# Tiles of x turned in memory ahead of time: the cross-attention scores read them by DMA, without transposes on TensorE

## The chip, the core and the metric

The kernel runs on one core of one Trainium2 chip. The metric is the device time of one launch in microseconds (us), as the median of several runs; less is better. The core's engines run side by side, each with an instruction queue of its own: TensorE (PE; its weight loads are PEld), VectorE (DVE), ScalarE (ACT), GpSimd (POOL) and SyncE (SP), which in this kernel only issues DMAs. They wait for each other by semaphores.

## What is computed

Eight batches of x (512 rows of 512 numbers) go through a cross attention over 77 context rows and then through a layer of 16 attention experts. Cut to what matters (`ln` is a layer norm over the row):

```python
ctx = ctx_1024                                           # (8, 77, 512)
s   = einsum('bqd,bkd->bqk', ln(x), ctx) / sqrt(512)
att = softmax(where(mask, -1e9, s), -1)
x   = x + swapaxes(att @ ctx, -1, -2) @ W_merge.T + b_merge
h   = ln(x)
rw  = gating(h)                                          # (8*512, 16) expert weights per row, in sequences of 512
q, k, v = [sum_e rw[.., e] * (h @ proj_e) for proj in (q_proj, k_proj, v_proj)]   # 64 wide
a   = causal_softmax(q k^T / 8) @ v
out = x + sum_e rw[.., e] * (a @ o_proj_e)
```

All products are taken in two parts: a tile `hi` rounded to the matmul's number format and a tile `lo` that holds the rest, as hi*hi + hi*lo + lo*hi.

## The kernel before

The rows of x are cut into 32 tiles of 128 rows, four to a batch. The main loop goes batch by batch (`body(b, ...)`); a batch has 32 slots k, eight to a tile (j, g = k // 8, k % 8). In slot k, TensorE first multiplies a tile of h with the projections of two experts (a **group**: 12 matmuls, L1213), and then does the small jobs that tables of numbers place in this slot: transposes, scores, values, mixing, output projection. Each engine's program is the same walk over the slots, so the tables set the order on every engine. Bodies for batches 0, 1, 6 and 7 are written out; one loop runs batches 2 to 5; a last body finishes the attention of batch 7. A small ramp ahead of the loop does the cross attention of the first five tiles and loads the weights.

The cross attention runs five tiles ahead (`X1_LEAD`). For one tile the steps are:

- SP loads the rows of x into H (`load_x1`, L393) as soon as TensorE has turned the h that lay in H (slot 6 of the tile before); the mask follows on L394.
- TensorE turns H, four transposes of 128x128 into one of two psum banks psT (`move_rows`, L1131, slot 0); ScalarE copies the bank to hT_hi (`copy_rows`, L615, slot 0) and VectorE takes bank minus hT_hi as hT_lo (`low_rows`, helper `lo`, L793, slot 0). L1131, L615 and L793 serve h in slot 6 of each tile in the same way.
- VectorE takes mean and variance from H in slot 3. TensorE forms the scores from hT and the turned context in slot 4 (`x1_score`, L1146 and L1148). Softmax and the low parts follow in slots 4 to 6.

The next tile of h is prepared in the same slots: `sum_x2` on TensorE and `add_x2` on VectorE (slot 2, L1163, L863), `row_stats` (slot 2, L868 and L870), powers on POOL (L504 to L515), `normalise` into H (slot 4, L874), transposes of H (slot 6).

For the batch after this one TensorE sums G = att^T times the merge weights, one quarter q in each of the slots 17, 19, 21 and 23 (`sum_G`, L1154). The merge weights come from a scratch in memory by DMA into one pair of buffers (`load_merge`, L400): the quarter q+1 is loaded when quarter q has been summed. SP walks the slots as well and waits in order. In slot 19 it first waits for `row_stats` of this tile (L383, store of X2), issues that store, a slice of the context (L379) and the next context (L448), and only then the merge load; in slot 21 it first waits for `normalise` (L387) and loads X2.

Of the kernel before, what the change touches and what calls it, by code (L numbers as in the profile page):

```python
# [37 lines left out]
QK_T_AT = {15: 0, 18: 1, 31: 2, 2: 3}  # L38
SCORES_AT = {18: 0, 20: 1, 2: 2, 4: 3}
GATES_AT = {19: 0, 21: 1, 3: 2, 5: 3}  # L40
PROBS_T_AT = {20: 0, 22: 1, 4: 2, 6: 3}
GATES_T_AT = {24: 0, 8: 1}
VALUES_AT = {24: 0, 8: 1}
MIX_AT = {26: (0, 0), 27: (0, 1), 28: (0, 2), 29: (0, 3),
          10: (1, 0), 11: (1, 1), 12: (1, 2), 13: (1, 3)}
MIX_LO_AT = {k + 1: job for k, job in MIX_AT.items()}
PROJECT_AT = {k + 2: job for k, job in MIX_AT.items()}
Y_AT = {31: 0, 0: 1, 15: 2, 16: 3}
# [5 lines left out]
X1_T_SLOT, X1_MOMENTS_SLOT, X1_SCORE_SLOT, X1_INV_SLOT, X1_LOW_SLOT = 0, 3, 4, 5, 6  # L54
# [42 lines left out]
def cross_attention_then_experts_kernel(nc, x, ctx_in, mask, merge_t, bias, sim, gates, w_qkv, w_o, out):  # L97
# [21 lines left out]
    with whole:  # L119
# [15 lines left out]
        with ExitStack() as under:  # L135
# [8 lines left out]
            cs_raw = raw("cs_raw", [CP, P])  # L144
        W_lo_over = sb("Wqkv_lo", [P, KC * W_CHUNK], F32R)
# [5 lines left out]
        cs_lo_over = sb("cs_lo", [CP, P], F32R)  # L151

# [32 lines left out]
        hT = [pair(f"hT{p}", [P, D]) for p in range(2)]  # L185
# [36 lines left out]
        x_first = [X2[:], resid[0][:], resid[1][:], spare_wo[:, 6, :], spare_wo[:, 5, :]]  # L222
        merge_first = ([mixedT[n // 2][:, n % 2 * 2:n % 2 * 2 + 2, :].rearrange("p c l -> p (c l)") for n in range(4)],
# [13 lines left out]
        ld_x = [sem(f"ld_x{n}") for n in range(X1_LEAD)]  # L237
        ld_mask = sem("ld_mask")
# [15 lines left out]
        x1_in = sem("x1_in")  # L254
# [27 lines left out]
        MOVES, HIS, OWN_STEPS = 36, 20, 4 * (3 + 5) + 4  # L282
# [38 lines left out]
        def tile_copies(k, qkv, lead):  # L321

            if k in QK_T_AT and (lead if k <= LATE_QK else qkv):
                return QK_T_AT[k]
            return None

        def bank_jobs(k, b, qkv, lead):


            j, g, prepare, cross, attn, ab = job_lists(k, b, qkv, lead)  # L330
            return ["probs"] * (attn and k in PROBS_T_AT) + ["x1"] * (cross and g == X1_T_SLOT) + [
                "sum"] * (prepare and g == SUM_SLOT) + ["score"] * (cross and g == X1_SCORE_SLOT) + [
                "h"] * (prepare and g == H_T_SLOT) + ["qk"] * (tile_copies(k, qkv, lead) is not None) + [
                "gates"] * (attn and k in GATES_T_AT) + ["ctx"] * (2 * (qkv and k == CTX_T_AT and live(b + 2, B))) + [
                "mix"] * (attn and k in MIX_AT)

# [24 lines left out]

        with nc.Block() as block:
            @block.sync
            def _(sp):
                moves = Seq()
                sp.dma_start(ctx_first[0], ctx_in[0]).then_inc(ld_ctx[0], 16)
                for n in range(TILES):
                    sp.dma_start(x_first[n], row(x, n)).then_inc(ld_x[n], 16)
# [43 lines left out]
                load_slice(0, 0)  # L412
                sp.dma_start(x_first[TILES], row(x, TILES)).then_inc(ld_x[TILES], 16)
# [13 lines left out]
                for _ in range(16):  # L427
# [7 lines left out]
                def body(b, qkv, lead):  # L435
                    for k in range(SLOTS):
                        j, g, prepare, cross, attn, ab = job_lists(k, b, qkv, lead)
                        t = TILES * b + j
                        for job in bank_jobs(k, b, qkv, lead):
                            n = moves.step()  # L440
                            if job == "h" and cross and live(t + X1_LEAD + 1, N_TILES):
# [35 lines left out]
            def _(pool):  # L477
# [91 lines left out]
                def body(b, qkv, lead):  # L569
                    for k in range(SLOTS):  # L570
# [12 lines left out]
                        if attn and k in GATES_AT:  # L583

                            i = GATES_AT[k]
# [785 lines left out]
```

## Time and profile before

| what | value |
|---|---|
| median of 3 runs | 947.69 us (947.27 to 949.32) |
| the profiled execution, its own time | 950.48 us |
| its span, first to last instruction | 948.8 us |
| TensorE busy, share of the span | 913.8 us, 96% |
| VectorE busy | 648.4 us, 68% |
| ScalarE busy | 213.4 us, 22% |
| mean granted TensorE clock, of full speed | 0.98 |
| matmuls of all kinds | 5128 |

The profile is one execution, taken by the hardware profiler. Busy times are unions, so matmuls that overlap in the pipeline count once. In the rows, L12 is line 12 of the kernel before; an arrow in brackets at the end of a row says for how long the engine had been idle and what released it. A row that names several instructions merges them.

### The profile page before, as it was taken

What the parts mean: (1) busy time and instruction counts of PE and PEld (TensorE: products, weight loads), DVE (VectorE), ACT (ScalarE), POOL (GpSimd) and SP (SyncE); (2) the same over time, 40 slices, a digit from 0 to 9 for tenths busy, and PEclk for the clock granted to TensorE, in tenths of its full rate; (3) what the DMA queues carried; (4) which work ended last, traced back from release to release, by engine and by line L of the source; (5) the groups of instructions that cost most, each with busy time, mean ns of one, the idle gap of its engine ahead of it and who ended that gap; (6) DMA issues with size and microseconds to landing.
All of it is one profiled execution on the core that took longest, in us unless ns stands there. A gap on an engine that the chain in (4) does not pass through costs nothing.

```text
span 948.8 us, 16504 instructions
## 1 busy us (share of the span) xinstructions
PE 913.8 (96%) x5128; PEld 853.4 (90%) x5128; DVE 648.4 (68%) x1964; ACT 213.4 (22%) x554; POOL 133.8 (14%) x383
## 2 busy tenths in 40 slices
PE   6779999999999999999999999999999999999987
PEld 5679899999999999999999999999999999999976
DVE  6778777767586675867667576876758676665743
ACT  4522321212122121212212131211312121121111
POOL 3243111101111110111111011110101110010100
PEclk9789999999999999999999999999999999999997
DMA  8821411224120331114111141112312131010110
GB/s 270 327 59 36 154 33 38 61 65 131 48 69 26 97 103 47 58 37 148 49 48 57 39 159 35 66 39 69 130 34 69 36 112 48 36 51 31 35 45 22
DMA packets 46086, 71.57 MB, mean 75 GB/s; under 512 B 9529, under 2 KB 16089, under 8 KB 45762
## 3 DMA queue, kind: packets, MB, share of 16 engines
q1 hardware_dynamic: 46018, 70.80, 22.9%
q8 instruction: 26, 0.43, 0.2%
q14 instruction: 42, 0.34, 0.1%
HBM read 51.90 MB, written 18.87 MB: 75 GB/s over the span
## 4 chain that ended last, share of the span: by engine, by line
PE 77%; DVE 8%; issue 6%; DMA 5%; SPq 2%; DVEq 1%; POOLq 1%; POOL 1%; ACT 0%; ACTq 0%
PE psQ L1213 44%; PE psO L1318 10%; PE psM L1318 9%; DMA merge_lo<-merge_scratch 3%; PE psT L1131 2%; PE psO L1154 2%; PE psM L1293 2%; PE psT L1163 2%; PE psT L1261 2%; DMA MASK<-in_mask 2%; DVE acc L919 1%; PE psT L1146 1%; DVE neg_mx L1036 1%; DVE b_stats L868 1%; PE psT L1240 1%
## 5 line engine op out<-in xcount | busy, mean ns | idle before, releaser
L1213 PE MATMUL psQ<-Wqkv_hi,hT_hi 128*128 128x384 f32 (+1 forms) x1024 | 350.7, 342 | 5.0 <-DVE hT_lo L793 2.9
L1213 PE MATMUL psQ<-Wqkv_lo,hT_hi 128*128 128x384 f32 (+1 forms) x1024 | 348.8, 341 | 0.0
L1213 PE MATMUL psQ<-Wqkv_hi,hT_lo 128*128 128x384 f32 (+1 forms) x1024 | 348.1, 340 | 0.0
L919 DVE SCALAR_TENSOR_TENSOR acc<-psQ,RW,acc 128x192 f32<-128x192 f32 x448 | 164.1, 411 | 145.5 <-PE psQ L1213 144.1
L1213 PEld LDWEIGHTS psQ<-Wqkv_hi,hT_hi 128*128 128x128 f32 x1024 | 194.5, 190 | 10.9 <-DVE hT_lo L793 3.3
L1213 PEld LDWEIGHTS psQ<-Wqkv_lo,hT_hi 128*128 128x128 f32 x1024 | 194.2, 190 | 4.3
L1213 PEld LDWEIGHTS psQ<-Wqkv_hi,hT_lo 128*128 128x128 f32 x1024 | 194.2, 190 | 0.0
L504 POOL TENSOR_TENSOR pow_tmp<-b_mv,eps 128x1 f32<-128x1 f32 x32 | 7.5, 236 | 659.3 <-DVE b_mv L870 659.3
L751 ACT ACTIVATE mixedT_hi<-mixed_f 128x512 fp32r<-128x512 f32 x64 | 40.5, 632 | 241.6 <-DVE mixed_f L1088 172.3
L615 ACT ACTIVATE hT_hi<-psT 128x512 fp32r<-128x512 f32 x64 | 38.2, 597 | 142.1 <-PE psT L1131 141.6
L1318 PE MATMUL psO<-Wo_hi,mixedT_hi 128*128 128x512 f32 x128 | 53.7, 419 | 0.7 <-DVE mixedT_lo L1078 0.7
L793 DVE TENSOR_TENSOR hT_lo<-psT,hT_hi 128x512 fp32r<-128x512 f32 x64 | 44.0, 688 | 10.5 <-ACT hT_hi L615 9.3
L1318 PE MATMUL psO<-Wo_hi,mixedT_lo 128*128 128x512 f32 x128 | 51.1, 399 | 0.0
L1318 PE MATMUL psO<-Wo_lo,mixedT_hi 128*128 128x512 f32 x128 | 50.9, 398 | 0.0
L1318 PE MATMUL psM<-Wo_hi,mixedT_lo 128*128 128x512 f32 x128 | 50.8, 397 | 0.0
L1318 PE MATMUL psM<-Wo_hi,mixedT_hi 128*128 128x512 f32 x128 | 50.8, 397 | 0.0
L1318 PE MATMUL psM<-Wo_lo,mixedT_hi 128*128 128x512 f32 x128 | 50.7, 396 | 0.0
L1078 DVE TENSOR_TENSOR mixedT_lo<-mixed_f,mixedT_hi 128x512 fp32r<-128x512 f32 x64 | 43.6, 682 | 6.4 <-ACT mixedT_hi L751 6.4
L1088 DVE TENSOR_TENSOR mixed_f<-psT,attT 128x512 f32<-128x512 f32 x64 | 43.7, 683 | 3.1 <-PE psT L1261 3.1
L729 ACT ACTIVATE qkT<-psT 128x256 fp32r<-128x256 f32 x32 | 12.3, 385 | 138.3 <-PE psT L1240 138.3
L879 DVE SCALAR_TENSOR_TENSOR logit<-psQ,pow_out,neg_sig 128x16 f32<-128x16 f32 x32 | 7.5, 234 | 49.3 <-PE psQ L1213 49.3
L1131 PE MATMUL psT<-ident,H 128*128 128x128 f32 x236 | 36.1, 276 | 5.1 <-DVE H L874 3.2
(187 smaller groups left out, 1331.8 us busy)
## 6 DMA issues: line engine op xcount, KB each, us to landing
X<-in_x SPq DMA_DIRECT2D x32, 256.0 KB, 2.7
x_scratch<-X SPq DMA_DIRECT2D x32, 256.0 KB, 2.0
resid<-x_scratch SPq DMA_DIRECT2D x32, 256.0 KB, 3.9
out<-resid SPq DMA_DIRECT2D x32, 256.0 KB, 2.0
merge_hi<-merge_scratch SPq DMA_DIRECT2D x28, 256.0 KB, 2.9
merge_lo<-merge_scratch SPq DMA_DIRECT2D x28, 256.0 KB, 3.4
H<-in_x SPq DMA_DIRECT2D x27, 256.0 KB, 2.8
W_raw<-in_w_qkv SPq DMA_DIRECT2D x8, 768.0 KB, 10.5
```

The lines of the kernel that those rows point to most:

```text
L615: act.activation(hT[p][0][:], psT[moves.bank()][:], ACT.Copy).then_inc(moved_hi, 1)
L751: act.activation(mixedT[0][:, 2 * (u % 2):2 * (u % 2) + 2, :], mixed_f[u % 2][:], ACT.Copy).then_inc(mix_hi, 1)
L793: dve.tensor_tensor(dst, src, dst_hi.bitcast(F32), ALU.subtract).then_inc(moved_lo, 1)
L919: dve.scalar_tensor_tensor(out=acc[e][:], in0=src, scalar=w, in1=acc[e][:], op0=ALU.mult, op1=ALU.add).then_inc(expert_added, 1)
L1078: dve.tensor_tensor(mixedT[1][:, 2 * (u % 2):2 * (u % 2) + 2, :], mixed_f[u % 2][:], mixedT[0][:, 2 * (u % 2):2 * (u % 2) + 2, :].bitcast( ...
L1088: dve.tensor_tensor(mixed_f[u % 2][:], psT[moves.bank()][:].rearrange("p (c l) -> p c l", c=2), attT[:].unsqueeze(1).broadcast_to([P, 2, 2 ...
L1131: last = pe.transpose(bank[:, c * P:(c + 1) * P], tile[:, c * P:(c + 1) * P], ident[:])
L1154: last = pe.matmul(psO[0:CP, :], a[:, q, :], w, start=(q == 0 and n == 0), stop=(q == TILES - 1 and n == 2))
L1163: last = pe.matmul(bank[:], a[:], w[:], start=(n == 0), stop=(n == 2))
L1213: last = pe.matmul(psQ[g % 4][:, 0:first_col(g) + PW], a[:, c * P:(c + 1) * P], w[:, c, E + g * PW - first_col(g):E + (g + 1) * PW], start ...
L1261: last = pe.matmul(bank[:, s * 2 * P:(s + 1) * 2 * P], spread[:, 2 * u + s, :], gatesT[:], start=True, stop=True)
L1318: last = pe.matmul((psO, psM)[i][:], a[:, 2 * (u % 2) + c, place(i)], w[:, 2 * u + c, :], start=(u == 0 and c == 0 and n == 0), stop=(u == ...
```

## The change

The host lays out a second copy of x, `x_t`, in which every 128-row tile is turned in blocks of 128 columns, just as hT holds it. SP loads a turned tile by a plain DMA of 128 rows of 2 KB into a new buffer XT, which lies in the same memory as hT_lo. ScalarE copies XT to hT_hi and VectorE subtracts hT_hi from XT in place, which leaves hT_lo. The 32 times four transposes of x on TensorE are gone. The rows of x are still loaded into H, for the mean and the variance. In the ramp five turned tiles are loaded ahead of or beside the tiles of x.

The split of a turned tile stands in slot 2 of its tile, ahead of `add_x2` on VectorE, where the split of the transposes' bank stood in slot 0. `load_xt` stands on SP at the head of slot 0 (its first call, for batch 0, in the ramp), and waits until all groups of the tile before are done, since XT and hT_lo of that parity were in use until then.

The tables of slots were also rewritten: pairs of tables, one for the last batch, with late slots written as 34 for 2 and so on, read by a function `job`. Both tables of each pair hold the same numbers and these are the numbers of before, so no other job moves; only the count of bank moves per batch falls from 36 to 32.

```diff
-X1_T_SLOT, X1_MOMENTS_SLOT, X1_SCORE_SLOT, X1_INV_SLOT, X1_LOW_SLOT = 0, 3, 4, 5, 6
+X1_HIGH_SLOT, X1_MOMENTS_SLOT, X1_SCORE_SLOT, X1_INV_SLOT, X1_LOW_SLOT = 2, 3, 4, 5, 6
...
+            XT = [raw(f"XT{p}", [P, D]) for p in range(2)]
...
+        hT_lo_over = [sb(f"hT{p}_lo", [P, D], F32R) for p in range(2)]
...
+        xt_first = [XT[0][:], XT[1][:], probs[0][:], probs[1][:], spare_wo[:, 4, :]]
...
-        MOVES, HIS, OWN_STEPS = 36, 20, 4 * (3 + 5) + 4
+        MOVES, HIS, OWN_STEPS = 32, 16, 4 * (3 + 5) + 4
...
                 for n in range(TILES):
+                    sp.dma_start(xt_first[n], turned(n)).then_inc(ld_xt[n], 16)
                     sp.dma_start(x_first[n], row(x, n)).then_inc(ld_x[n], 16)
...
+                def load_xt(t, p):
+
+                    if isinstance(t, int) and t == 0:
+                        sp.wait_ge(x1_max_ready, TILES)
+                    else:
+                        sp.wait_ge(qkv_summed, PAIRS * t)
+                    sp.dma_start(XT[p][:], turned(t + X1_LEAD)).then_inc(xt_in, 16)
...
+                        if cross and g == 0 and not (is_first(b) and j == 0):
+                            load_xt(t, (j + 1) % 2)
...
+                def turned_high(t1, p):
+
+                    if isinstance(t1, int) and t1 < X1_LEAD:
+                        act.wait_ge(ld_xt[t1], 16)
+                        src = xt_first[t1]
+                    else:
+                        act.wait_ge(xt_in, 16 * (t1 - X1_LEAD + 1))
+                        src = XT[p][:]
+                    act.activation(hT[p][0][:], src, ACT.Copy).then_inc(xt_hi, 1)
...
-                        if cross and g == X1_T_SLOT:
-                            copy_rows(p1)
+                        if cross and g == X1_HIGH_SLOT:
+                            turned_high(t1, p1)
...
+                def turned_low(t1, p):
+
+                    dve.wait_ge(xt_hi, t1 + 1)
+                    src = xt_first[t1] if isinstance(t1, int) and t1 < X1_LEAD else XT[p][:]
+                    dve.tensor_tensor(hT[p][1][:], src, hT[p][0][:].bitcast(F32), ALU.subtract).then_inc(xt_lo, 1)
...
-                        if cross and g == X1_T_SLOT:
-                            low_rows(p1)
+                        if cross and g == X1_HIGH_SLOT:
+                            turned_low(t1, p1)
...
-                        if cross and g == X1_T_SLOT:
-                            move_rows(H, x1_in, 32 * (t + 1))
-                            x1_moved = moves.now()
```

VectorE in the loop, slots 16 to 18, before (`logit` opens slot 16, `weight` slot 17, and `neg_mx` is the row maximum of the scores in slot 18; `link` waits and register work are left out):

```order
L1031 TENSOR_TENSOR resid<-psM,resid 128x512
...
L793 TENSOR_TENSOR hT_lo<-psT,hT_hi 128x512
L895 SCALAR_TENSOR_TENSOR weight<-logit,gate_exp 128x16
...
L1036 TENSOR_REDUCE neg_mx<-psM 128x1
...
L863 TENSOR_TENSOR X<-psT,X 128x512
...
L868 BN_STATS b_stats<-X 128x6
```

and now:

```order
L1092 TENSOR_TENSOR resid<-psM,resid 128x512
L956 SCALAR_TENSOR_TENSOR weight<-logit,gate_exp 128x16
...
L1097 TENSOR_REDUCE neg_mx<-psM 128x1
...
L857 TENSOR_TENSOR hT_lo<-XT,hT_hi 128x512
...
L924 TENSOR_TENSOR X<-psT,X 128x512
...
L929 BN_STATS b_stats<-X 128x6
```

The subtraction has moved from ahead of the gate weights to a place behind the row maximum and ahead of `add_x2` and `row_stats`.

SP from slot 14 of batch 1 on, before (the last row stands in slot 21):

```order
L393 DMA H<-in_x 128x512
L394 DMA MASK<-in_mask 128x77
L409 DMA out<-resid 128x512
L400 DMA merge_hi<-merge_scratch 128x512
L400 DMA merge_lo<-merge_scratch 128x512
L409 DMA out<-resid 128x512
L383 DMA x_scratch<-X 128x512
L379 DMA cs_raw<-in_ctx_in 77x128
L448 DMA ctx_raw<-in_ctx_in 77x512
L400 DMA merge_hi<-merge_scratch 128x512
L400 DMA merge_lo<-merge_scratch 128x512
L388 DMA X<-in_x 128x512
```

and now:

```order
L426 DMA H<-in_x 128x512
L427 DMA MASK<-in_mask 128x77
L435 DMA XT<-in_x_t 128x512
L450 DMA out<-resid 128x512
L441 DMA merge_hi<-merge_scratch 128x512
L441 DMA merge_lo<-merge_scratch 128x512
L450 DMA out<-resid 128x512
L416 DMA x_scratch<-X 128x512
L412 DMA cs_raw<-in_ctx_in 77x128
L493 DMA ctx_raw<-in_ctx_in 77x512
L441 DMA merge_hi<-merge_scratch 128x512
L441 DMA merge_lo<-merge_scratch 128x512
```

One DMA is added at the head of slot 16; the store of X2 still stands ahead of the merge load of slot 19.

## Rows read from the trace of the kernel before

**Rows 1.** The page's first part: busy time, share of the span, instructions.
```profile
PE 913.8 (96%) x5128; PEld 853.4 (90%) x5128; DVE 648.4 (68%) x1964; ACT 213.4 (22%) x554; POOL 133.8 (14%) x383
```

**Rows 2.** Stretches: their us, busy us (instructions) per engine, clock, DMA share, GB/s.
```profile
110.00:140.00 30.00, 28.11 (x156) 26.30 (x155) 19.27 (x58) 5.73 (x15) 3.36 (x10) 0.94 0.20 71
...
400.00:500.00 100.00, 99.79 (x569) 93.34 (x569) 68.84 (x210) 20.51 (x56) 14.16 (x43) 1.00 0.21 67
```

**Rows 3.** TensorE in order of time (start, us), around one turn of x in slot 16.
```profile
484.89 0.34 PE L1213 MATMUL psQ<-Wqkv_hi,hT_lo 128*128 128x400 f32 x1
485.07 0.60 PE L1131 MATMUL psT<-ident,H 128*128 128x128 f32 x4
485.42 0.42 PE L1213 MATMUL psQ<-Wqkv_hi,hT_hi 128*128 128x384 f32 x1
485.68 0.33 PE L1213 MATMUL psQ<-Wqkv_lo,hT_hi 128*128 128x384 f32 x1
```

**Rows 4.** Waits by engine and line: us in total, times, longest us.
```profile
PE psO L1154 <- DMA merge_lo<-merge_scratch: 3.1, 6, 1.9
...
PE psT L1131 <- DMA MASK<-in_mask: 1.9, 4, 0.7
```

**Rows 5.** VectorE in order of time, batch 3: slots 18 and 26.
```profile
435.22 0.29 DVE L1036 TENSOR_REDUCE neg_mx<-psM 128x1 f32<-128x128 f32 x1 [0.34 <-PE psM L1277]
...
435.65 0.69 DVE L863 TENSOR_TENSOR X<-psT,X 128x512 f32<-128x512 f32 x1
436.26 0.28 DVE L1058 TENSOR_TENSOR kT_lo<-psT,qkT 128x128 fp32r<-128x128 f32 x1
...
437.85 0.18 DVE L870 BATCH_NORM_AGGREGATE b_mv<-b_stats 128x2 f32<-128x6 f32 x1
...
459.24 0.68 DVE L863 TENSOR_TENSOR X<-psT,X 128x512 f32<-128x512 f32 x1
```

**Rows 6.** SP's DMA issues in order of time, batch 3: slots 19 and 23.
```profile
438.06 0.34 SPq L383 DMA_DIRECT2D x_scratch<-X  x1
...
439.94 0.43 SPq L400 DMA_DIRECT2D merge_lo<-merge_scratch  x1
...
450.92 0.43 SPq L400 DMA_DIRECT2D merge_lo<-merge_scratch  x1
```

**Rows 7.** The tile merge_lo: time from issue to landing of its loads.
```profile
DMA to landing us min/median/max: 2.9/3.4/5.9
```

**Rows 8.** TensorE in order of time: sums of G in slot 21, batches 2 and 3.
```profile
332.24 0.42 PE L1154 MATMUL psO<-merge_hi,att_hi 128*78 128x512 f32 x1 [0.20 <-DMA merge_lo<-merge_scratch]
...
443.42 0.41 PE L1154 MATMUL psO<-merge_hi,att_hi 128*78 128x512 f32 x1
```

**Rows 9.** VectorE and TensorE in order of time: batch 0, slots 1 and 6.
```profile
48.14 1.76 DVE L846 TENSOR_TENSOR Wqkv_lo<-W_raw,Wqkv_hi 128x1536 fp32r<-128x1536 f32 x1 [0.56 <-ACT Wqkv_hi L634]
...
64.36 0.63 PE L1131 MATMUL psT<-ident,H 128*128 128x128 f32 x4 [3.21 <-DVE H L874]
```

**Rows 10.** The chain that ended last, in order of time, end of batch 0.
```profile
113.21 1.29 PE psO L1154 x3
114.50 3.33 PE psQ L1213 x12
...
126.64 2.09 PE psQ L1213 x12
```

**Rows 11.** The page's DMA issues: count, KB each, median us from issue to landing.
```profile
H<-in_x SPq DMA_DIRECT2D x27, 256.0 KB, 2.8
W_raw<-in_w_qkv SPq DMA_DIRECT2D x8, 768.0 KB, 10.5
```

**Rows 12.** The tile merge_raw: ns min/median/max of the ramp's split with an SBUF source.
```profile
L638 ACT ACTIVATE mixedT_hi<-merge_raw x2: 612/612/613, 13.8 to 17.0; 128x512 fp32r<-128x512 f32 x2
L851 DVE TENSOR_TENSOR qkT<-merge_raw,mixedT_hi x2: 673/678/684, 19.0 to 19.7; 128x512 fp32r<-128x512 f32 x2
```

**Rows 13.** VectorE in order of time: its first read of scores in the ramp.
```profile
10.88 0.22 DVE L817 COPY sc<-psT 128x77 f32<-128x77 f32 x1
```

More of the change, by code:

```diff
@@ L94, in products, with cross_attention_then_experts_kernel @@
     return ((a[0], b[0]), (a[0], b[1]), (a[1], b[0]))
-def cross_attention_then_experts_kernel(nc, x, ctx_in, mask, merge_t, bias, sim, gates, w_qkv, w_o, out):
+def cross_attention_then_experts_kernel(nc, x, x_t, ctx_in, mask, merge_t, bias, sim, gates, w_qkv, w_o, out):
     B, S, D = x.shape
@@ L184, in cross_attention_then_experts_kernel @@
         H = sb("H", [P, D])
-        hT = [pair(f"hT{p}", [P, D]) for p in range(2)]
+        hT = [(sb(f"hT{p}_hi", [P, D], F32R), hT_lo_over[p]) for p in range(2)]
         acc = [sb(f"acc{k}", [P, Q3]) for k in range(2)]
@@ L237, in cross_attention_then_experts_kernel @@
         ld_x = [sem(f"ld_x{n}") for n in range(X1_LEAD)]
+        ld_xt = [sem(f"ld_xt{n}") for n in range(X1_LEAD)]
         ld_mask = sem("ld_mask")
@@ L319, in first_col, with last_batch, job, tile_copies @@
             return E if g == 0 else 0
[L321 to L325, printed above, removed]
+        def last_batch(ab):
+            return isinstance(ab, int) and ab == B - 1
+        def job(places, k, b):
+            own = k >= LEAD
+            at = places[last_batch(b if own else b - 1)]
+            return at.get(k if own else SLOTS + k)
+        def tile_copies(k, b, qkv, lead):
+            late = k <= LATE_QK
+            if not (lead if late else qkv):
+                return None
+            return QK_T_AT[last_batch(b - 1 if late else b)].get(SLOTS + k if late else k)
         def bank_jobs(k, b, qkv, lead):
             j, g, prepare, cross, attn, ab = job_lists(k, b, qkv, lead)
[L331 to L335, printed above, removed]
+            return (["probs"] * (attn and job(PROBS_T_AT, k, b) is not None)
+                    + ["sum"] * (prepare and g == SUM_SLOT)
+                    + ["score"] * (cross and g == X1_SCORE_SLOT)
+                    + ["h"] * (prepare and g == H_T_SLOT)
+                    + ["qk"] * (tile_copies(k, b, qkv, lead) is not None)
+                    + ["gates"] * (attn and job(GATES_T_AT, k, b) is not None)
+                    + ["ctx"] * (2 * (qkv and k == CTX_T_AT and live(b + 2, B)))
+                    + ["mix"] * (attn and job(MIX_AT, k, b) is not None))
         def place(i):
@@ L426, in _ @@
                 load_x2(1)
-                for _ in range(16):
+                load_xt(0, 1)
+                for _ in range(11):
                     n = moves.step()
@@ L582, in body @@
                             spread_part((5, 7, 13, 15).index(k))
-                        if attn and k in GATES_AT:
-                            i = GATES_AT[k]
+                        if attn and job(GATES_AT, k, b) is not None:
+                            i = job(GATES_AT, k, b)
                             a = TILES * ab + i
@@ L744, in body @@
                             G_high(b + 1)
-                        if attn and k in MIX_AT:
-                            h, u = MIX_AT[k]
+                        if attn and job(MIX_AT, k, b) is not None:
+                            h, u = job(MIX_AT, k, b)
                             m = 8 * ab + 4 * h + u
@@ L1103, in body @@
                             slice_low(t + 2)
-                        if attn and k in GATES_AT:
-                            i = GATES_AT[k]
+                        if attn and job(GATES_AT, k, b) is not None:
+                            i = job(GATES_AT, k, b)
                             a = TILES * ab + i
@@ L1185, in _ @@
                 move_ctx(ctx_first[1], 1)
-                move_rows(x_first[TILES], ld_x[TILES], 32)
-                x1_score(0, moves.now())
+                x1_score(TILES, 0)
                 move_rows(H, h_ready, 1)
@@ L1263, in body @@
                             last.then_inc(moved, 1)
-                        if attn and k in SCORES_AT:
-                            i = SCORES_AT[k]
+                        if attn and job(SCORES_AT, k, b) is not None:
+                            i = job(SCORES_AT, k, b)
                             if i % 2 == 1:
@@ L1314, in body @@
                             pe.wait_ge(mix_lo, 4 * h2 + u + 1)
-                            for i in range(2):
+                            for i in parts:
                                 for c in range(2):
```

138 lines of the change are left out of this document (72 added, 66 removed), and 3 rows, old and new, of the table MIX_AT.

## The prediction

> **What bounds the kernel now.** I read the page's first part first: TensorE is busy 96% of the span, VectorE 68% [rows 1]. Such shares are averages, so the stretches come next. From 400 to 500 us TensorE is busy 99.79 of 100 us at the full granted clock, VectorE 69 us [rows 2]: from the end of batch 0 to the tail of batch 7, each us taken off TensorE's queue is a us off the span, as long as nobody else becomes late. In batch 0 it is otherwise. TensorE waits 3.21 us for h [rows 9] and 1.9 us for a DMA at 113 us [rows 4, 10], and what it saves ahead of such a wait turns into more waiting. Last I read the waits that TensorE has in the full regime, for the load of H with its mask ahead of the turn of x and for the merge weights ahead of sums of G [rows 4]. They are short, but they tell which releasers have no slack left.
>
> **The bursts of four transposes.** One turn of x begins at 485.07 and the next group at 485.42; the group's second matmul comes 0.26 us after its first, where the usual distance is that from 484.89 to 485.07, 0.18 [rows 3]. A burst costs 0.35 + 0.08 to 0.09 = 0.44 us, and not four times the length of one transpose, since they overlap in the pipeline. There are 27 in the body, one for each load of H [rows 11]: four to each of batches 0 to 5 and three in batch 6. Those of slots 8 and 24 stand ahead of the gates' transposes and I price them alike. The three of slots 0, 8 and 16 of batch 0 lie ahead of the wait at 113.21, whose end a DMA sets; they give nothing. 24 x 0.44 = 10.6 us off.
>
> The Trainium skill (VectorE: DVE Perf Modes, section "The three transpose paths") gives 390 ns for one 128x128 bf16 transpose on TensorE, and advises TensorE for that size when psum will do. As an estimate by that page, 24 bursts of four would be worth 37 us. The trace disagrees for these f32 tiles in a full pipeline [rows 3], and the row decides.
>
> **The waits for H.** TensorE no longer reads x from H, and VectorE needs it only in slot 3. The 1.9 us of waits [rows 4] go, and with four of them a slower start of the burst, which I put at 0.1 us in all: 2.0 us off. Next in line stand the gates' transposes, whose inputs are due two slots earlier, so nothing else is late there.
>
> **ScalarE and VectorE.** Each does the same copy and the same subtraction, from XT instead of psum. The nearest rows for a source outside psum are the ramp's merge weights, 612 and 678 ns [rows 12]; VectorE's read of psum for the same 128x512 takes 0.69 us [rows 5]. Equal, cost nothing. What counts is the place. Where VectorE has a backlog from slot 0 to 2, out of slot 0 and into slot 2 cancel, and `add_x2` stays where it is. Where it catches up with TensorE in between, all that follows the new place is later. That is so in slot 18: VectorE reaches the row maximum 0.34 us before TensorE has the scores [rows 5]. In the changed kernel it arrives 0.6 us earlier, idles longer, and then the subtraction takes 0.61 us from start to start (as 435.65 to 436.26 [rows 5]); `add_x2` and `row_stats` end 0.61 us later as seen from TensorE. In slot 10 the same may happen; behind it waits the mixing of slots 10 to 13, which TensorE takes up two slots later, so I put it at nothing (bound: 0.6 us for each of 6 batches, part of the fourth rival).
>
> **Who waits for slot 18.** SP in slot 19 waits for `row_stats`: it ends at 438.03, the store of X2 is issued at 438.06, and behind it and two more the merge load, its second half at 439.94 [rows 5, 6]. With the median landing of 3.4 us [rows 7] that is there at 443.34; TensorE comes for it at 443.42 without a wait in batch 3, and waits 0.20 us in batch 2 [rows 8]. There is no slack. So in batches 1 to 5 the sum of G in slot 21 waits longer: by 0.61 in the batches in which it already waited (2, 4 and 5), by 0.61 less some 0.15 in the others (1 and 3): 3 x 0.61 + 2 x 0.46 = 2.8 us. The load for slot 23 hangs on `normalise`, which moves by less, and TensorE comes later for it; so the waits there, 0.6 us of the 3.1 (less 1.9 at 113 us and three of 0.2 in slot 21 [rows 4, 8]), vanish. In batch 6 SP loads no further context ahead of it and has slack. Sum: 2.2 us on. The ends: 0, if SP was held by something else, and 0.61 x 6 = 3.7, if all of it adds.
>
> **The load of XT.** A load of the same size lands in 2.8 us [rows 11]. Its latest issue, as seen from its use, is in slot 24, behind the merge load at 450.92 [rows 6]: at about 451.4, lands at 454.2, is copied by 454.8, and VectorE comes for it at 459.2, where `add_x2` now is [rows 5]. It brings 27 x 256 KB more where the DMA engines are busy 0.21 of the time [rows 2]. Cost: nothing. If that cover of 4.4 us were gone, VectorE would stop in slot 26 (third rival).
>
> **Batch 0.** After the subtraction in slot 0 VectorE idles 0.56 us for ScalarE's copy of W [rows 9], so taking it out gains nothing there; in slot 2 it pushes `add_x2`, the powers on POOL, `normalise` and the transposes of h, for which TensorE already waits [rows 9]. 0.7 us on; nothing less, since every step is in series. In the next tiles of this batch VectorE is behind throughout, and out and in cancel.
>
> **The ramp.** Five turns leave TensorE, but x now lands behind the turned tiles, and VectorE takes the moments of a tile before its low part. It reads the first scores at 10.88 [rows 13]. From the order of loads I estimate 10.6; the small loads for the gates and the merge weights land 2 to 4 us later and may hold ScalarE or VectorE. Bounds: 2 us off, 2.5 us on; I take 0.3 off.
>
> **Sum.** -10.6 - 2.0 + 2.2 + 0.7 - 0.3 = -10.0 us. The profiled execution took 950.48 us with a span of 948.8: the execution should come out at 940.5, the span at 938.8. The median of the runs, 947.69, lies 2.8 below that execution; the same 10.0 off it gives 937.7.
>
> **Rivals.** First, the merge load does not get later, because SP was held by TensorE's own sum in slot 19, which ends within 0.1 us of `row_stats`. Then 10.6 + 2.0 + 0.3 = 12.9 are gained, 934.8, and if batch 0 follows, 27 x 0.44 + 2.0 + 1.2 (the old merge waits) = 15.1, or 932.6. Against it: the load is issued only 1.9 us after `row_stats` and two other DMAs stand between them, so every delay of the store is handed on.
>
> Second, the stalls of slot 21 lower the granted clock. After the 1.89 us wait at 113.21 it fell (0.94 over 110 to 140 us [rows 2]), and a group took 3.33 us instead of 2.09 and the sum of G 1.29 instead of 0.7 [rows 10]: 1.8 us lost. The new stalls are 0.5 to 0.8 us, between the old ones of up to 0.7 [rows 4], behind which the clock stayed, and this one. Five falls cost 9 us: 946.7, no change that can be told.
>
> Third, on the other side: XT is late for slot 26. From its issue at 451.4, the copy and the 459.2 above, VectorE waits as soon as a landing takes over 7.2 us, and if TensorE has no slack behind it, the 10.0 us are gone when slot 26 of six batches loses 1.7 us each, at a landing of 8.9. At the 10.5 us of the weights' loads in the ramp [rows 11] it is 3.3 us late, 6 x 3.3 = 20 us: 957.5. For it: the issue stands behind two merge loads. Against: the DMA share of 0.21 [rows 2] and landings of 2.8 to 3.4.
>
> Fourth, the main term holds, but the ramp, slot 10 or the merge chain cost 2 to 5 us more: 940 to 943.
>
> That the change does not do what it says is excluded: TensorE's order has 128 transposes fewer and nothing in their place.
>
> **How the numbers follow.** Forecast 0.62, first rival 0.15, second 0.07, third 0.02, fourth 0.14. The range is 933.5 to 943: it holds the forecast, the near end of the first rival and the fourth. A measurement of this kernel tells a change from none at about 0.2% (1.9 us). Faster by more than that: forecast, first, fourth and some of the second, 0.94. Within: 0.04. Slower: 0.02.
>
> **What the new profile would show.** 128 matmuls fewer, and 128 transposes from H where there were 236. No wait of TensorE for the mask's DMA. VectorE idle some 0.9 us ahead of the row maximum of slot 18. The wait of the sums of G for merge loads up from 3.1 to 5 or 6 us, in slot 21 0.4 to 0.9 each. XT landing in about 2.8 us, with no wait of VectorE in slot 2, 10, 18 or 26 for ScalarE's copy. The first group of the body 0.3 us earlier. I am wrong if TensorE waits in the body for ScalarE or VectorE where it did not, if the clock falls once per batch, or if the first group starts more than 2 us later.

## The result

| kernel | median | runs |
|---|---|---|
| before | 947.71 us | 947.27 to 949.32, 4 runs |
| changed | 937.35 us | 934.89 to 938.53, 4 runs |

The ratio is 0.9884, with a 95% interval of 0.9859 to 0.991: 10.4 us faster, where 10.0 was forecast (937.7). The profiled execution of the changed kernel took 938.53 us with a span of 935.5. So the two medians differ by 10.4 us, the two profiled executions by 11.95 and their spans by 13.3. Where these 3 us between the readings come from is a question of the experiments.

The page's first part of the changed kernel, the counterpart of [rows 1]:

```profile
PE 895.0 (96%) x5000; PEld 835.9 (89%) x5000; DVE 646.3 (69%) x1964; ACT 214.7 (23%) x554; POOL 136.8 (15%) x383
```

128 matmuls fewer, 18.8 us of busy time less on TensorE, and the other engines within 3 us of before. The stretches, as in [rows 2] (us, busy us and instructions per engine, clock, DMA share, GB/s):

```profile
110.00:140.00 30.00, 28.75 (x164) 26.75 (x163) 21.40 (x62) 7.11 (x19) 3.84 (x10) 1.00 0.26 85
400.00:500.00 100.00, 99.40 (x568) 92.90 (x568) 69.46 (x220) 22.45 (x62) 12.96 (x39) 1.00 0.28 85
```

Two things have changed. From 110 to 140 us the granted clock is 1.00, where it was 0.94. And in the hundred microseconds of the loop TensorE now stands idle for 0.60 us, where it was 0.21. The waits of TensorE, by line (us in total, times, longest), against [rows 4]:

```profile
PE psO L1215 <- DMA merge_lo<-merge_scratch: 4.8, 7, 1.2
```

The row for the mask's DMA is gone. The wait for merge weights has grown from 3.1 to 4.8 us. TensorE at these places, in order of time (start, us; the idle time ahead in brackets), the end of batch 0 and slot 21 of batches 2 and 3, against [rows 8, 10]:

```profile
113.02 0.43 PE L1215 MATMUL psO<-merge_hi,att_hi 128*78 128x512 f32 x1 [1.25 <-DMA merge_lo<-merge_scratch]
...
326.54 0.45 PE L1215 MATMUL psO<-merge_hi,att_hi 128*78 128x512 f32 x1 [0.77 <-DMA merge_lo<-merge_scratch]
...
436.48 0.45 PE L1215 MATMUL psO<-merge_hi,att_hi 128*78 128x512 f32 x1 [0.60 <-DMA merge_lo<-merge_scratch]
```

Batches 1, 4, 5 and 6 wait 0.35, 0.63, 0.67 and 0.55 us in the same slot. VectorE in slot 18 of batch 3, against [rows 5]:

```profile
427.51 0.29 DVE L1097 TENSOR_REDUCE neg_mx<-psM 128x1 f32<-128x128 f32 x1 [0.37 <-PE psM L1329]
427.83 0.15 DVE L1099 TENSOR_SCALAR neg_mx<-neg_mx 128x1 f32<-128x1 f32 x1
427.93 0.69 DVE L857 TENSOR_TENSOR hT_lo<-XT,hT_hi 128x512 fp32r<-128x512 f32 x1
428.54 0.68 DVE L924 TENSOR_TENSOR X<-psT,X 128x512 f32<-128x512 f32 x1
...
430.73 0.18 DVE L931 BATCH_NORM_AGGREGATE b_mv<-b_stats 128x2 f32<-128x6 f32 x1
```

From the row maximum to the end of the row statistics it is 3.40 us, against 438.03 - 435.22 = 2.81 before: 0.59 more. SP follows (L416 stores X2 once the statistics are there, L441 loads the merge weights), against [rows 6]:

```profile
430.94 0.34 SPq L416 DMA_DIRECT2D x_scratch<-X  x1
...
432.83 0.43 SPq L441 DMA_DIRECT2D merge_lo<-merge_scratch  x1
```

The order of events is that of the prediction: 430.91 statistics, 430.94 store, 432.83 second half of the merge load, and TensorE waits for its landing until 436.48. To see where the gain lies I subtract, group by group, the start in one kernel from the start in the other. The gain of the changed kernel over the one before, at the first group of each batch, is 0.17 us (batch 0), 2.18, 4.05, 6.03, 7.78, 9.90, 12.08 and 12.70 (batch 7), and 13.2 at the end. Within a batch a burst shows as a step of 0.35 to 0.49, slot 8 of batches 2 to 5 as 0.83 to 1.28, and from slot 20 to 22 0.4 to 0.84 us are lost again. From the first group of batch 1 to that of batch 7 it is 668.08 us before and 657.56 now: 10.5 of the 13.2 us lie there, 2.0 in batch 0.

### The profile page after: what moved, and what is told of

Its sections match the earlier page's. It is cut to its first block, busy times and chain, and to the rows that moved or that the text cites. A ratio compares the mean times of both kernels' runs of the same rounds, so it can differ in the third digit from the quotient of the medians.

```text
span 935.5 us, 16276 instructions
## 1 busy us (share of the span) xinstructions
PE 895.0 (96%) x5000; PEld 835.9 (89%) x5000; DVE 646.3 (69%) x1964; ACT 214.7 (23%) x554; POOL 136.8 (15%) x383
## 4 chain that ended last, share of the span: by engine, by line
PE 84%; DVE 4%; issue 4%; DMA 3%; POOLq 1%; SPq 1%; POOL 1%; DVEq 1%; ACT 0%
PE psQ L1268 50%; PE psO L1370 10%; PE psM L1370 9%; DMA merge_lo<-merge_scratch 3%; PE psO L1215 2%; PE psT L1224 2%; PE psM L1345 2%; PE psT L1313 2%; PE psT L1192 1%; PE psT L1207 1%; PE psT L1276 1%; PE psT L1292 1%; PE psT L1209 1%; PE psM L1329 1%; DVE X L924 1%
## 5 line engine op out<-in xcount | busy, mean ns | idle before, releaser
L806 ACT ACTIVATE mixedT_hi<-mixed_f 128x512 fp32r<-128x512 f32 x64 | 40.5, 632 | 229.5 <-DVE mixed_f L1149 164.3
L1207 PE MATMUL psT<-ctxT,hT_hi 128*128 128x156 f32 x128 | 34.3, 335 | 9.6 <-DVE hT_lo L857 9.6
L1207 PEld LDWEIGHTS psT<-ctxT,hT_hi 128*128 128x128 f32 x128 | 27.1, 212 | 10.7 <-issue 8.0
L1209 PE MATMUL psT<-ctxT,hT_lo 128*128 128x78 f32 x128 | 31.6, 257 | 0.0
```

What stands on the lines that cost most here:

```text
L806: act.activation(mixedT[0][:, 2 * (u % 2):2 * (u % 2) + 2, :], mixed_f[u % 2][:], ACT.Copy).then_inc(mix_hi, 1)
L1207: pe.matmul(bank[:, 0:2 * CP], high, ctxT[:, c, :, :].rearrange("p a k -> p (a k)"), start=(c == 0), stop=False, skip_group_check=True)
L1209: last = pe.matmul(bank[:, 0:CP], low, ctxT[:, c, 0, :], start=False, stop=(c == KC - 1), skip_group_check=True)
```

## Experiments

Four kernels ran on one chip beside the kernel before (946.99 us, 9 runs), eight on another, in two groups of four (before: 946.13 us, 25 runs; 947.19 us, 10 runs). One is the changed kernel again; two ask whether a burst is worth what I priced, three whether the new waits hang on VectorE's order or on SP's, four what lowers the clock at the end of batch 0, and two how much cover XT has.

**The changed kernel again.**

> The changed kernel once more, as the measure for the three runs beside it on the same chip. Its first profiled execution had a span of 935.5 us, 13.3 under the one before, where the medians of the runs differ by 10.4. Either reading has a price: if the profiled execution before was a slow one of its kind, the ratio here is again near 0.989 (937.3 against 947.7 us); if the changed kernel varies more by itself, its runs spread over more than 3 us (934.9 to 938.5 so far). TensorE should wait for merge loads about 4.8 us in 7 places, once 1.25 us near 113 us, with the granted clock full from 70 us to the tail of batch 7.

Median 935.64 us (934.94 to 937.35), ratio 0.9877 (0.9857 to 0.9897), near the first one. In its trace the merge loads cost 4.4 us in seven places, but not in the same ones: at the end of batch 0 slot 21 waits 0.49 us and slot 23 nothing, and slot 21 of batch 3 waits 1.39 us. From batch 1 to batch 7 it takes 658.51 us, 9.6 less than the kernel before. The landing of one and the same load differs between the two executions by more than a microsecond (4.29 and 2.87 us for that of slot 21 in batch 3). A difference at one place in two traces, below that, proves little; the sum over six batches does.

**The bursts alone.** In both kernels, behind the first group of a tile:

```diff
+                        if cross and g == 0:
+                            if not isinstance(b, int) or n >= 3:
+                                pe.wait_ge(expert_added, 2 * (n - 2))
+                            pe.wait_ge(x1_in, 32 * (t + 1))          # turns_h alone
+                            for c in range(KC):
+                                pe.transpose(psQ[1][:, c * P:(c + 1) * P], ident[:], ident[:])   # turns_h: H
```

> The changed kernel with work added that nothing reads: in the slots where the kernel before turned a tile of x, 27 in the body, TensorE turns the identity four times into a free psQ bank, and waits for no new input. It prices the bursts alone. My theory: 0.44 us each where the pipeline is full, 24 of them on the path (three of batch 0 lie ahead of a wait for a DMA): 10.6 us more than the changed kernel, up to 11.9 if all 27 count. A rival: the bursts were cheaper (0.27 us, three steps of the pipeline) and the rest of the gain was waits and clock; then 6.5 us more.

Median 946.40 us (10 runs), against 936.30 of the changed kernel with one wait that cost nothing (delay_b0, below, same chip): 10.1 us. TensorE around the burst of slot 16, batch 3, against [rows 3]:

```profile
426.14 0.34 PE L1268 MATMUL psQ<-Wqkv_hi,hT_lo 128*128 128x400 f32 x1
426.32 0.60 PE L1284 MATMUL psQ<-ident 128*128 128x128 f32 x4
426.68 0.42 PE L1268 MATMUL psQ<-Wqkv_hi,hT_hi 128*128 128x384 f32 x1
426.93 0.34 PE L1268 MATMUL psQ<-Wqkv_lo,hT_hi 128*128 128x384 f32 x1
```

Subtracting starts, the steps of a batch are 0.41, 0.40, 0.41 and 0.45 us, 1.67 in all, in every batch from 1 to 5; the 24 bursts that I counted come to 10.0 us where I had 10.6. The main term stands and was 6% too large. The estimate that the Trainium skill leads to (VectorE: DVE Perf Modes, "The three transpose paths", 390 ns for one 128x128 bf16 transpose) counts that figure four times; the trace again shows less: here four f32 ones in a full pipeline take 0.40 to 0.45 us together.

> The same, but TensorE turns H (the rows of x) and waits for the load of H and of the mask first, as the kernel before did; nothing reads the result. The difference to the run with the identity is the waits for H and the mask. My theory: 2.0 to 2.6 us (0.5 us in each slot 8 of batches 2 to 5 and a slower start), so 12.6 to 13.2 us more than the changed kernel. If these waits only came from something else of the kernel before, the two runs agree within 0.5 us.

Median 950.42 us (10 runs), 4.0 more than with the identity, where 2.0 to 2.6 were expected. The waits by line, in its trace, show them by name:

```profile
PE psQ L1285 <- DMA MASK<-in_mask: 3.9, 5, 1.4
```

By group starts, slot 8 of batches 2 to 5 loses 1.22, 0.58, 0.83 and 0.74 us, 3.4 together. The waits for H and mask are real, a cost of their own, and larger than the 2.0 I took from the rows: I read 1.9 us off the profile of before and added 0.1, where the comparison of the first two traces already gives 2.6. The 3.4 can't be carried over to the kernel before as it stands, since turns_h has the loads of XT as well.

**Who delays the merge load.** One edit on VectorE, one on SP, and both.

```diff
-                        if cross and g == X1_HIGH_SLOT:
-                            turned_low(t1, p1)
...
                             row_stats(x2_moved)
+                        if cross and g == X1_HIGH_SLOT:
+                            turned_low(t1, p1)
```

> Only VectorE's order differs: the subtraction that makes hT_lo of x stands behind the row statistics of the same slot and not ahead of add_x2. My theory of the new waits in slot 21 (0.35, 0.77, 0.60, 0.63, 0.67 and 0.55 us in batches 1 to 6) is that the row statistics of slot 18 end 0.61 us later, SP stores X2 later, and the merge load behind that store lands later. Then each wait shrinks by up to 0.61: 0.35 + 0.61 + 0.60 + 0.61 + 0.61 + 0.55 = 3.3 us, and tile 0 of batch 0, where TensorE waits 3.77 us for h, gives another 0.6 to 0.7: 4.0 us less than the changed kernel, a span of 931.5 and runs near 933.4. The rival is that SP was held by TensorE's own sum in slot 19 and by landings that became longer: then the waits of slot 21 stay at 0.5 to 0.7 each and only batch 0 gains, 0.7 us in all, 936.7.

Median 931.18 us (929.96 to 934.73), 4.5 less than the changed kernel beside it. Its waits by line, and VectorE and SP in slots 18 and 19 of batch 3:

```profile
PE psO L1215 <- DMA merge_lo<-merge_scratch: 2.1, 3, 0.8
```

```profile
425.67 0.29 DVE L1097 TENSOR_REDUCE neg_mx<-psM 128x1 f32<-128x128 f32 x1 [0.37 <-PE psM L1329]
...
428.38 0.18 DVE L931 BATCH_NORM_AGGREGATE b_mv<-b_stats 128x2 f32<-128x6 f32 x1
428.49 0.69 DVE L857 TENSOR_TENSOR hT_lo<-XT,hT_hi 128x512 fp32r<-128x512 f32 x1
```

```profile
428.59 0.34 SPq L416 DMA_DIRECT2D x_scratch<-X  x1
...
430.49 0.43 SPq L441 DMA_DIRECT2D merge_lo<-merge_scratch  x1
```

From the row maximum the statistics end after 2.89 us (3.40 before this edit) and the merge load is issued after 4.82 (5.32): both half a microsecond earlier, and the waits fall from 4.4 to 2.1 us. An order on VectorE, of an instruction that nobody waits for there, is felt on TensorE through SP. The first rival of the prediction, SP held by TensorE's own sum, would have left the waits as they were.

```diff
+                        if qkv and k in G_AT:          # moved here, ahead of keep_x2 and load_x2
+                            n = TILES * b + G_AT[k] + 1
+                            if live(n, N_TILES - TILES):
+                                load_merge(n, (G_AT[k] + 1) % TILES)
                         if prepare and g == SUM_SLOT + 1:
                             keep_x2(t + 1)
```

> Only SP's order differs: in slots 17, 19 and 21 the load of the next merge quarter stands ahead of the store of X2, the loads of the context and the load of X2. By my theory the merge load then hangs only on TensorE's sum two slots before: in slot 19 it is issued about 2 us earlier (in batch 3 at 430.8 instead of 432.8), in slot 21 of batch 0 about 0.75 earlier. The six waits of slot 21 (3.6 us) vanish and the one near 113 us falls from 1.25 to 0.5: 4.3 us less than the changed kernel, a span of 931.2 and runs near 933.0. If the waits came from the landing itself or from the sum in slot 19, they stay, and the time does (937.3). If the later store of X2 makes the load of X2 late for slot 26, VectorE waits there for that DMA, and the kernel gains less or loses.

Median 931.78 us (930.57 to 933.09), 3.9 less. No wait of TensorE for a merge load is left in its trace (4.3 us less and 933.0 were expected). SP in slot 19 of batch 3:

```profile
428.87 0.42 SPq L441 DMA_DIRECT2D merge_lo<-merge_scratch  x1
429.45 0.34 SPq L416 DMA_DIRECT2D x_scratch<-X  x1
```

The row maximum is at 425.65 here, so the load now follows it by 3.22 us and not 5.32. X2 stored a little later costs nothing that shows: VectorE waits for no load of X2 in the body.

> Both edits: the subtraction behind the row statistics and the merge load first on SP. If the waits of slot 21 are one chain (row statistics, SP, merge load), each edit cures it alone and the gains don't add: 3.6 for the six waits, 0.75 near 113 us and 0.7 for h in batch 0, together 5.0 us less than the changed kernel, a span of 930.5 and runs near 932.3. If they add (4.0 + 4.3), the span would be 927.2 and the runs near 929.0.

Median 929.72 us (928.23 to 930.65), ratio to before 0.981 (0.9792 to 0.9828), 5.9 less than the changed kernel: the gains of 4.5 and 3.9 don't add, which is one chain cut at two places. The traces say the same of batches 1 to 6: 658.5 us in the changed kernel run again, 655.4 in split_late, 652.8 in merge_first and 653.4 with both. There SP's edit alone gives all that the pair gives (and more than the 3.9 us of waits that it removes from these batches; the rest is open). What the pair has over SP's edit alone in the medians, 2.1 us, lies ahead of batch 1 in the traces. One part of it is the wait for h of tile 0, the row beside [rows 9], 2.13 us here, 3.87 in merge_first and 3.77 in the changed kernel:

```profile
64.82 0.63 PE L1192 MATMUL psT<-ident,H 128*128 128x128 f32 x4 [2.13 <-DVE H L935]
```

How much of that is VectorE's edit isn't shown: stall_one (below), which has VectorE's order unchanged, waits 1.04 us at this place. This is the fastest of all the kernels run, 17.3 us under the one before.

**The clock at the end of batch 0.** In the trace of before, the sum of G at 113.21 waits 1.89 us and the clock falls behind it; in the changed kernel it waits 1.25 and the clock stays. Three kernels set the size of this stall by holding SP's merge load in slot 21 of batch 0 until a later event, and one takes the stall out of the kernel before.

```diff
+                                if is_first(b) and k == 21:
+                                    sp.wait_ge(qkv_summed, 23)                # delay_b0
+                                    sp.wait_ge(moved, moves.now() + 2)        # stall_one
+                                    sp.wait_ge(moved_lo, moves.now() + 2)     # stall_two
                                 load_merge(n, (G_AT[k] + 1) % TILES)
```

> The changed kernel with one wait more on SP: the merge load of slot 21 of batch 0 is held until TensorE has done the group of slot 22, about 1.2 us. So TensorE's stall near 113 us grows from 1.25 to about 2.4 us; nothing else differs. If the stall lowers the granted clock, as I read it in the kernel before (a stall of 1.89 us, then 3.4 us at the lower level), the groups behind it take 3.3 us instead of 2.1 for some 3.4 us: 1.2 + 1.8 = 3.0 us more than the changed kernel. If the fall had another cause, only the 1.2 us are lost and the clock stays full behind the stall.

It missed: the load came 1.9 us behind the load of X, yet landed soon enough for a stall of 0.36 us, and the median is 936.30 us. It tells nothing of the clock, but something of the landing. The second half of this merge load took 2.86 us here, and 2.94 and 2.93 in the two kernels that follow, where SP holds it longer still. In the eight traces in which it follows the load of X within 1.2 us it took 3.65 to 5.90 us (5.90 before, 4.98 and 4.06 in the two of the changed kernel). So the delay itself seems to have taken away some of the stall that it was to make. That the load of X just ahead of it is the reason isn't shown: with SP's order turned round the load took 2.93 us (merge_first) and 2.92 (both), but 4.40 in before_merge_first.

> Once more the stall at the end of batch 0, since a delay of the merge load to 107.96 us left a stall of only 0.36 us (its landing took 3 us and not 5). Here SP holds the load until TensorE has turned h in slot 22, about 109.1 us in the trace of the changed kernel: issued to 109.9, landed at 112.9 to 113.3, a stall of 1.5 to 2.2 us like the 1.89 of the kernel before. If a stall of this size lowers the clock, the profile shows 3.4 us at the lower level behind it and the run is 1.8 us longer than its stall explains (in all 3.3 to 4 us over the changed kernel without any stall there, 1.5 to 2.2 if the clock stays).

Again smaller than meant: 1.10 us, clock 1.00 behind it, median 936.65 us.

> The same, held until VectorE has made hT_lo of that h (about 110.0 us): a stall of 2.4 to 2.9 us. If the stall of 1.89 us lowered the clock in the kernel before, this one must too: 3.4 us at the lower level, 1.8 us lost, 4.2 to 4.7 us over a kernel without a stall there. If the clock stays, the fall in the kernel before was not the stall's.

Here the stall is 2.44 us, in the profiled execution. Stretches of 4 us behind it, first of this kernel, then of stall_one, then of the kernel before:

```profile
114.00:118.00 4.00, 3.92 (x12) 3.48 (x13) 0.00 (x0) 0.00 (x0) 0.00 (x0) 0.57 0.73 228
```

```profile
111.00:115.00 4.00, 3.41 (x20) 3.19 (x21) 1.85 (x6) 0.08 (x1) 0.00 (x0) 1.00 0.90 284
```

```profile
113.00:117.00 4.00, 3.79 (x12) 3.44 (x13) 0.48 (x3) 0.00 (x0) 0.00 (x0) 0.57 0.27 102
```

TensorE begins 12 matmuls in 4 us at a mean granted clock of 0.57, which is most of the stretch at the lower level of 1.2 GHz (0.50), and 20 at the full one. From the start of the group of slot 22 to that of slot 25, stall_two takes 4.1 us more than the changed kernel run again, which has no stall in slot 23: 2.44 for the stall, and 1.65 for the clock, close to the 1.8 read from before. The median doesn't show the second part. It is 938.24 us, 1.6 over stall_one and 1.9 over delay_b0, hardly more than the longer stall alone (1.3 and 2.1), where 4.2 to 4.7 over a kernel without a stall was expected. The profiled execution took 940.73 us and the other three 937.65 to 938.28; whether the clock fell in those, no trace shows.

Behind a stall the clock can fall, then, and behind the one of 1.89 us in the kernel before it did. Does its size decide? The two kernels with XT later (below) have more such stalls, most of them in slot 21. Here are two of about the same size in xt_two_later, the group behind the stall of 2.38 us in batch 3 and that behind the 2.56 us in batch 4:

```profile
446.50:450.00 3.50, 3.50 (x23) 3.34 (x22) 1.65 (x8) 2.31 (x8) 0.24 (x1) 1.00 0.54 182
```

```profile
558.00:562.00 4.00, 4.00 (x13) 3.56 (x14) 0.94 (x5) 1.78 (x6) 0.24 (x1) 0.57 0.56 162
```

In xt_two_later the clock fell behind 2.39, 2.46 and 2.56 us and stayed behind 1.81, 2.26 and 2.38; in xt_three_later it fell behind 2.33, 2.47, 2.86 and 2.97 and stayed behind 1.80, 1.90, 2.15, 2.36 and 2.51. With before and stall_two that is nine falls for seventeen stalls between 1.80 and 2.97 us, and none behind any stall under 1.80 in the full regime, 1.39 us of the changed kernel among them. The longer ones have more of the falls: one of the five stalls from 1.80 to 2.15 us, two of the five from 2.26 to 2.39, six of the seven from 2.44 on. What decides beside the size is open; by these counts a stall of 1.89 us costs the 1.8 us more in one case of a few, and the trace of before holds such a case.

The last of the four is the kernel before with SP's edit of merge_first and nothing else.

> The kernel before, with only SP's order changed: the load of the next merge quarter ahead of the store and the load of X2. The stall near 113 us shrinks from 1.89 by about 0.5 to 1.4 us, the five short waits (1.2 us in all) vanish. If a stall of that size no longer lowers the clock, another 1.8 us or so come back: 3.5 us less than the kernel before. If the clock falls all the same, 1.7 us less.

Median 943.71 us (10 runs) against 946.13: 2.4 less, ratio 0.9967 (0.9949 to 0.9985). That is 1.4 to 4.8 us, which holds both the 3.5 and the 1.7 of the expectation. In the trace the stall is gone, not halved, and the clock stays; it gains 3.5 us at the end of batch 0 over the trace of before, and 6.8 by its end. Trace against trace gives almost three times what median against median does. The profiled execution of before is thus a long one of its kind, as its 950.48 us beside a median of 947.69 already said; that its stall at 113 us has a part in it is likely, though the other executions have no trace to show it. What they do have is their mean granted clock. Of the 44 executions of the kernel before on the two chips of the experiments, the six at 0.980 or less took 949.3 us in the median, the 18 at 0.986 or more 945.4. The profiled execution stands at 0.980, among those that were longest at the lower level; at which place the others differ, this number doesn't say.

**XT later.**

```diff
-                        sp.wait_ge(qkv_summed, PAIRS * t)
+                        sp.wait_ge(qkv_summed, PAIRS * t + 2)     # 3 in xt_three_later
...
-                        if cross and g == 0 and not (is_first(b) and j == 0):
+                        if cross and g == 2 and not (is_first(b) and j == 0):
```

> The changed kernel with each turned tile loaded two slots later: SP waits for the groups of slots 0 and 1 of the tile. In the trace of the changed kernel the shortest time from issue to VectorE's use is 7.05 us (slot 26), less 2.9 for landing and 0.62 for the copy: 3.5 us of cover. The issue moves by 4.0 us there, 5.8 in slot 10, 3.6 in slot 2, 7.1 in slot 18, so VectorE should wait 0.5 us in slots 10 and 26 and not in the others. My theory: TensorE feels little of it, within 1 us of the changed kernel. The third rival's view, that what VectorE loses in slot 26 is lost on TensorE too: 6 x 0.5 x 2 = 6 us more.

Median 955.51 us (7 runs), 8.3 slower than the kernel before on this chip and some 19 over the changed one. My expectation (within 1 us of the changed kernel, or 6 us more) was wrong in the slot and in the size. VectorE in slot 18, SP in slot 19 and TensorE in slot 21 of batch 3:

```profile
438.00 0.69 DVE L857 TENSOR_TENSOR hT_lo<-XT,hT_hi 128x512 fp32r<-128x512 f32 x1 [2.10 <-ACT hT_hi L670]
```

```profile
441.01 0.34 SPq L416 DMA_DIRECT2D x_scratch<-X  x1
...
442.86 0.43 SPq L441 DMA_DIRECT2D merge_lo<-merge_scratch  x1
```

```profile
446.18 0.45 PE L1215 MATMUL psO<-merge_hi,att_hi 128*78 128x512 f32 x1 [2.38 <-DMA merge_lo<-merge_scratch]
```

I had expected no wait in slot 18. VectorE waits 2.10 us there, and it is again the chain of the statistics: TensorE's wait for merge loads is 16.9 us in nine places, 12.5 more than in the changed kernel, and the three falls of the clock behind such waits come on top. In slots 10 and 26, where I expected the trouble, VectorE waits 0.2 to 0.5 us and TensorE not at all.

> The same, three slots later: VectorE should wait 2.6 us in slot 10, 2.5 in slot 26, 1.7 in slot 18 and 1.2 in slot 2. This stands for a landing of 9 us where 2.9 was measured. By the third rival of the prediction slot 26 hands its 2.5 us to TensorE in six batches, 15 us more, slower than the kernel before; slot 10 may add as much. If VectorE has slack behind these slots (the scores of slot 4, 12, 20 and 28 come two slots later, the mixing uses a copy two slots old), the cost is under 5 us.

Median 992.15 us, some 56 over the changed kernel, where 15 to 30 was the highest reading. The two largest waits of TensorE:

```profile
PE psT L1313 <- DVE X L924: 19.3, 12, 1.8
PE psO L1215 <- DMA merge_lo<-merge_scratch: 17.8, 8, 3.0
```

Now the mixing of slots 10 to 13 and 26 to 29 stands too, behind `add_x2`, 1.6 us each time. Four falls of the clock are in this trace too; what the 56 us are made of beyond these, I haven't added up. The guess that VectorE has slack in slots 10 and 26 holds for half a microsecond, and not for two and a half. So the third rival's mechanism is real; it was only far from its point, since XT lands in 2.5 to 5.0 us (median 2.9) and all of its waits were hidden.

## Why the prediction was right, point by point

**The bursts.** Forecast 10.6 for 24. Measured 10.0 by group starts; the medians give 10.1 for all 27, the traces of turns_ident and delay_b0 11.3 at the last group and 10.3 in the spans, so whether the three of batch 0 cost nothing isn't decided. Right; the 0.44 was the row of one burst, the mean is 0.42.

**The waits for H.** Forecast 2.0; 2.6 beyond the bursts in slot 8 of batches 2 to 5 between the first two traces, 3.4 in the kernel that has them back beside the loads of XT. Undersized by a quarter at least.

**The merge chain.** Forecast +2.2, and this the runs show, link by link: the statistics 0.59 later, the load with them, a wait in slot 21. From slot 20 to slot 24 the changed kernel loses 2.7 us against the one before over batches 1 to 6. What the step missed is batch 6, which I had declared free since SP loads no context there; it waits 0.55 us like the others. One sign of the prediction didn't come: VectorE idles 0.37 us ahead of the row maximum of slot 18 in batch 3, and not some 0.9. I had taken the subtraction out of VectorE's time and forgotten that the burst of slot 16 goes from TensorE's as well: from the gate logits of slot 16 to the row maximum it is 6.51 us before and 6.11 now. The step itself holds, since only the time behind the row maximum counts for it.

**ScalarE and VectorE.** Forecast nothing for the durations: the copy takes 619 ns and the subtraction 681, where 612 and 678 were read from the ramp. Slot 10 at nothing: TensorE has no wait there. Right.

**XT.** Forecast nothing, cover 4.4 us. The landing was right (median 2.9), and so was that TensorE and VectorE don't wait for it in the body; ScalarE does, up to 2.1 us in slot 26, at no cost. The cover was not tested by the change, and the late loads show that it is thinner in slot 18 than my working had it, and guards more than slot 26.

**Batch 0.** Forecast +0.7 for tile 0, and from slot 0 to slot 8 the changed kernel indeed loses 0.89. But the end of the batch, to which I gave nothing, gave back 2.3 us between the first two traces, 0.4 of it the burst of slot 24: the stall shrank from 1.89 to 1.25 and with it went the fall of the clock. I had this fall in my hands as the price of the second rival, 1.8 us, and used it only for falls that might be added, not for the one that might go. Since the stall's size differs between executions by more than 0.6 us, and the fall behind a stall of this size comes in some cases only, the medians need not contain all of it. That fits that 10.4 were gained there, which is what batches 1 to 6 alone gained in the traces (10.5, and 9.6 in the second trace of the changed kernel), and not 12 or 13; no trace of a median execution shows it.

**The ramp.** Forecast 0.3 off; the first group starts 0.17 earlier and the first scores are read at 10.52 us, against 10.88 [rows 13]. Neither confirmed nor refuted: in the traces of the kernels that share this ramp the first group starts anywhere from 37.8 to 40.5 us.

**The sum.** The errors: bursts 0.6 too much, waits for H 0.6 too little, merge chain 0.5 too little, ramp 0.1 too much, batch 0 some 2.3 too little in the traces and an unknown part of that in the medians. So measured the terms come to 11.7 us and the traces to 13.2; the other 1.5 lies in steps of under 0.1 us between the bursts of batches 1 to 6 (about 0.9 together), in batch 7 and in the tail, and had no term. That the total was within 0.4 us of the median is earned in the loop, where 9.9 was forecast for batches 1 to 6, and is luck in the rest: errors of 0.5 to 0.6 us cancelled, and the 2 us of batch 0 hardly show in the medians.

**The rivals.** The first (no later merge load) is refuted by split_late. The second (stalls of slot 21 lower the clock) did not come true: the clock is 1.00 through the loop with stalls of 0.35 to 0.77, and in one trace 1.39. The third is real at another size of delay. Of the fourth, only the half microsecond of the merge chain came.

## What to carry to other kernels

When an instruction is moved on an engine, follow each thing behind it through SP's queue as well: a subtraction that stood 0.6 us too early in VectorE's order and a store ahead of a load in SP's cost 4 to 6 us of the 17 to be had. Price a burst by the distance between the starts of its neighbours, not by its own length. And read a trace against the median of the runs first: where a profiled execution is 2.8 us over the median, one of its stalls may be a chance one, and a gain at that place can show in the traces and not in the times.

## What was not expected of the hardware

Landings of the same 256 KB load at the same place of the program took 3.65 to 5.90 us in eight traces with the load of X just ahead of it, 4.98 and 4.06 in two of one kernel, and 2.9 where SP held it back; a stall of TensorE was 1.89, 1.25 or nothing by it. Behind stalls of 1.80 to 2.97 us inside full work the clock fell in nine cases of seventeen, once in the five up to 2.15 us and six times in the seven from 2.44 on; a fall cost 1.65 us in the trace of stall_two. And a delay of 2.10 us on VectorE in slot 18 turned into 1.8 us more of TensorE's wait three slots later (2.38 against 0.60 in batch 3), through two engines and a DMA, without any slack on the way.
